# Store and load order on SyncE in the first stage of a fused Mamba and mixture-of-experts layer

## What is computed

```python
xn = _layernorm(x, axis=-1)
proj = jnp.einsum('bld,ed->ble', hidden_states, in_proj_w)
x, gate = jnp.split(proj, 2, axis=-1)
...                                   # causal convolution of x over 4 taps
xc = jax.nn.silu(xc + conv_b[None, :, None])
ssm = jnp.einsum('bld,ed->ble', xt, x_proj_w)
ts, Bm, Cm = jnp.split(ssm, [DT_RANK, DT_RANK + D_STATE], axis=-1)
...
y = y * jax.nn.silu(gate)             # after the scan
# router
logits = x @ gate_w.T
scores = jax.nn.softmax(logits, axis=-1)
topk_w, topk_i = jax.lax.top_k(scores, K)
...                                   # slot lists: which tokens each expert takes
```

## Time and profile before

| | |
|---|---|
| median of 3 runs | 1425.2 us (1420.97 to 1434.94) |
| profiled execution | 1420.89 us, its span 1418.7 us |
| mean granted PE clock | 0.971 |
| PE busy | 1317.4 us, 93% |
| DVE busy | 1083.4 us, 76% |
| ACT busy | 895.9 us, 63% |
| POOL busy | 880.8 us, 62% |
| DMA | 304.87 MB, mean 215 GB/s |

### The profile page before, as it was taken

The page is one execution under the profiler, slowest core; times in us unless marked ns, Lnnn a source line. Parts: engine busy times, 40 slices in busy tenths (PEclk is TensorE's granted clock), DMA queues, the critical chain, the costliest instruction groups (busy, mean ns, idle before and its releaser), DMA issues.

```text
span 1418.7 us, 53995 instructions
## 1 busy us (share of the span) xinstructions
PE 1317.4 (93%) x21895; PEld 813.1 (57%) x21895; DVE 1083.4 (76%) x1259; ACT 895.9 (63%) x1912; POOL 880.8 (62%) x523
## 2 busy tenths in 40 slices
PE   5898988769999999999999999999999869999998
PEld 3666656535555545555455555455554558787876
DVE  4688798749999979999789899889999255545554
ACT  3746554467878878887787878677786133333333
POOL 2444355269898978989789898888989130303030
PEclk9999999869999999999899999999999989999999
DMA  7152527558999999999889999989898732313130
GB/s 282 64 211 78 197 79 274 179 160 264 307 258 297 274 287 273 275 301 267 270 258 278 293 263 304 274 265 294 262 300 244 267 131 68 111 54 124 42 136 30
DMA packets 129681, 304.87 MB, mean 215 GB/s; under 512 B 18448, under 2 KB 20240, under 8 KB 127824
## 3 DMA queue, kind: packets, MB, share of 16 engines
q1 hardware_dynamic: 121984, 285.13, 61.5%
q0 software_dynamic: 7632, 18.91, 6.6%
HBM read 213.65 MB, written 56.77 MB: 191 GB/s over the span
## 4 chain that ended last, share of the span: by engine, by line
PE 40%; issue 19%; POOL 15%; DMA 2%; DVE 1%; ACT 1%; POOLq 1%; SPq 0%; DVEq 0%; ACTq 0%
PE p_dBx L1324 9%; PE p_dBx L1257 8%; POOL h_times_C L880 7%; POOL C_bcast L880 5%; PE p_y L1273 3%; PE p_y L1335 3%; PE p_g L1335 3%; PE p_u L1335 3%; PE p_g L1243 3%; PE p_dt L1335 2%; PE p_u L1226 2%; PE p_g L1226 2%; POOL moe L860 2%; DMA w_down_pair<-in_sw_down 1%; PE p_dt L1206 1%
## 5 line engine op out<-in xcount | busy, mean ns | idle before, releaser
L945 DVE TENSOR_TENSOR_SCAN state<-dA,state_carry,p_dBx 128x512 f32<-128x512 f32 x512 | 626.5, 1266 | 78.3 <-PE p_dBx L1257 69.3
L1091 ACT ACTIVATE dA<-dt_blocks,A_par 128x512 f32<-128x512 f32 x512 | 338.7, 709 | 39.3 <-DMA dt_blocks<-step_rows 39.2
L880 POOL TENSOR_TENSOR h_times_C<-state,C_bcast 128x1024 f32<-128x1024 f32 x128 | 305.2, 2385 | 70.8 <-DVE state L945 68.9
L880 POOL TENSOR_TENSOR C_bcast<-state,C_bcast 128x1024 f32<-128x1024 f32 x128 | 319.6, 2780 | 22.4 <-DVE state L945 17.5
L1257 PEld LDWEIGHTS p_dBx<-B_diagonals,step_rows 64*32 64x32 f32 x16384 | 232.4, 106 | 162.8 <-issue 162.7
L1257 PE MATMUL p_dBx<-B_diagonals,step_rows 64*32 64x128 f32 x16384 | 303.6, 276 | 10.3 <-issue 9.5
L254 POOL TENSOR_TENSOR w_in_parts_lo<-C_bcast,w_in_parts_hi 128x512 fp32r<-128x512 f32 x64 | 88.9, 1391 | 142.0 <-ACT w_in_parts_hi L447 141.7
L1324 PE MATMUL p_dBx<-x_parts,shared_w_parts 128*128 128x512 f32 (+1 forms) x576 | 139.7, 404 | 17.3 <-DVE shared_w_parts L974 12.1
L895 POOL TENSOR_TENSOR step_rows<-step_rows 128x512 f32<-128x512 f32 x16 | 20.6, 1319 | 202.2 <-DMA step_rows<-moe 202.2
L1324 PEld LDWEIGHTS p_dBx<-x_parts,shared_w_parts 128*128 128x128 f32 (+1 forms) x576 | 105.2, 184 | 51.8 <-issue 20.5
L326 DVE SCALAR_TENSOR_TENSOR conv_out<-conv_in,conv_w,conv_out 128x512 f32<-128x512 f32 x96 | 91.1, 958 | 9.4 <-ACT conv_out L461 7.1
(11 more groups left out here) (172 smaller groups left out, 2035.4 us busy)
## 6 DMA issues: line engine op xcount, KB each, us to landing
w_gate_pair<-in_w_gate SPq DMA_DIRECT2D x32, 1408.0 KB
w_up_pair<-in_w_up SPq DMA_DIRECT2D x32, 1408.0 KB, 8.1
w_down_pair<-in_w_down SPq DMA_DIRECT2D x66, 512.0 KB
dt_blocks<-step_rows SPq DMA_DIRECT2D x512, 64.0 KB
w_down_pair<-in_w_down SPq DMA_DIRECT2D x33, 384.0 KB
g_d<-y_gated SPq DMA_DIRECT2D x33, 256.0 KB, 4.3
sz_d<-silu_gate SPq DMA_DIRECT2D x32, 256.0 KB, 2.0
xt_d<-conv_out SPq DMA_DIRECT2D x4, 2048.0 KB, 7.3
```

Source lines behind the costliest of these rows:

```text
L880: pool.tensor_tensor(hc[m][:, b, :, :], hb[:, q, :, :], Cb[:, NM * cp + GS * m:NM * cp + GS * m + GS, :], ALU.mult).then_inc(s_hc, 1)
L945: ins = dve.tensor_tensor_scan(hb[:, g % NBUF, s, :], dA[:, g % NBUF, s, :], pB[:, g % 2, :].rearrange("p (t s) -> p s t", s=GS)[:, s, :], ...
L1091: ins = act.activation(dA[:, q, s, :], dtr[:, u, b, :], ACT.Exp, scale=A[:, bass.ds(d, 1), GS * g + s:GS * g + s + 1].rearrange("p a b -> ...
```

## The change

Only the order of SyncE's instructions in stage 1 changes. In each chunk, the stores of gate tiles 0 and 1 are issued ahead of the wait for the scores, and those of tiles 2 and 3 behind the `xn_d` store. In the last chunk the gate weights' load follows the stores of tiles 2 and 3, where it stood ahead of the stores of tiles 0 to 3; the 16 transfers of C are issued four at a time behind the stores of gate tiles 4, 5, 6 and 7, where all 16 stood ahead of them; and the up weights' load is issued behind all of these, directly ahead of the wait for the last chunk's `xt_d` store, where it stood behind the store of gate tile 3.

```diff
             for c in range(NCH):
                 sp.wait_ge(s_xnT, c + 1)
                 sp.dma_start(io["xnT_d"][c], xnT[:, :, :]).then_inc(s_xTs, 16)
+                store_gates(c, range(2))
                 sp.wait_ge(s_sc, c + 1)
                 sp.dma_start(xn_v[c], xs[:, :, :]).then_inc(s_xns, 16)
+                store_gates(c, range(2, ND // 2))
                 if c == NCH - 1:
                     tile_in.load_gate(sp, 0)
-                store_gates(c, range(ND // 2))
+                for d in range(ND // 2, ND):
+                    store_gates(c, range(d, d + 1))
+                    if c == NCH - 1:
+                        sp.wait_ge(s_wlo, 2 * ND * c + X_TURN)
+                        for a in range(2 * (d - ND // 2), 2 * (d - ND // 2) + 2):
+                            keep["load_C"](sp, 0, a)
                 if c == NCH - 1:
                     sp.wait_ge(s_val, NCH)
                     tile_in.load_up(sp, 0)
-                    sp.wait_ge(s_wlo, 2 * ND * c + X_TURN)
-                    for a in range(ND):
-                        keep["load_C"](sp, 0, a)
-                store_gates(c, range(ND // 2, ND))
                 sp.wait_ge(s_xt, ND * c + ND)
```

## The result

The change makes the kernel slower by 0.3%: the median is 1429.54 us (1423.86 to 1433.88, 20 runs) against 1423.24 us (1417.73 to 1435.8, 20 runs) for the kernel before. The ratio, 1.0032 with a 95% interval of 1.0016 to 1.0048, is that of the means (1429.28 and 1424.66); the medians lie 6.3 us apart. The profiled execution has a span of 1425.1 us (before 1418.7) and took 1427.25 us.

A forecast was written before the change was run, and what follows sets the result against it. VectorE was taken to set stage 1's chunks and the last `xt_d` store its end: +2.4 - 3.9 + 4.1, less up to 0.5, put the barrier +2.4 us later. On the median that gave 1427.6, stated as 1427.5; range 1416 to 1434.

The forecast's parts named there:

- DVE, not PE, sets the chunk's length: Stage 1: DVE runs nearly without a gap, so PE's gain is worth only what DVE can use.
- Part 1, the wait for the root: Chunks 2 and 3: DVE's wait for the reciprocal root falls to 1.14 us, by 1.65 and 1.62; together -3.3 us.
- Part 1, four meetings instead of two: Chunks 1 to 3, conv 2 to 4: two more GpSimd subtractions delay DVE, 2 x 0.9 = +1.8 us, to +2.1.
- Part 1 as a sum: Chunks 1 to 3, early gate stores: +1.9, +0.25 and +0.3 us, together +2.4; ends -3.3 and +3.0.
- a stop of 3 us or more before the transposes: Sign to see in the profile after: PE without a stall at n = 9 but with this stop.
- Part 2, the last chunk: ACT's 8.19 us and DVE's wait for the ranks go: -3.9 us at the `xt_d` store; ends -1.2 and -5.3.
- Part 3, the load in front of the store: Last chunk: up weights' load ahead of the last `xt_d` store, +4.1 us on its landing; ends 0 and +8.1.
- C's transfers and the gate weights' load cost nothing: Last chunk, SyncE's queue: C transfers between stores and the load behind gate stores 2 and 3 add nothing on the path.
- A: Rival: DVE's meetings with POOL stay two per chunk; -3.6 us, 1421.6; chance 0.22.
- B: Rival: meetings stay two per chunk and the up weights' load is hidden; -7.7 us, 1417.5; chance 0.06.
- C: Rival: SyncE's issues become the last chunk's chain, +2 to +4 us more, together about +6, 1431; chance 0.16.
- D: Rival: ACT's wait is for something other than the gate store; only +4.1 us remains, 1429.3; chance 0.04.

The follow-up runs named there:

- runs 5 and 6: Kernel before and changed kernel, GpSimd's subtractions in chunks 1 to 3 replaced by zero fills: 171.1 and 165.3 us from first exponent-sum to last; no ratio.
- Run 7: Changed kernel plus 36 identity transposes on PE ahead of the transposes of each chunk after the first: ratio 1.003 to the kernel before.
- run 12: The kernel before, unchanged, profiled once more: 191.6 us from first exponent-sum to last, then 48.8 to the barrier; timed once, no ratio.
- run 3: Changed kernel with the up weights' load moved directly behind the gate weights' load: ratio 0.999 to the kernel before, barrier at 285.75 us.
- run 11: Kernel before with only the last chunk's gate stores 0 and 1 early and gate weights' load behind tiles 2 and 3: ratio 0.9973.
- run 10: Same kernel as run 4, timed again: ratio 0.9988 to the kernel before (0.9971 to 1.0005), barrier at 283.63 us.
- run 4: Changed kernel with the old order in chunks 1 to 3 and the up weights' load behind the gate weights' load: ratio 0.9972 to the kernel before.

## Why the prediction was right, and where its terms were off

The forecast was 1427.5 us, 2.3 above the median known then, and the barrier 2.4 us later. The measured shift is +0.32%, 4.6 us, 2.3 to 6.8 by its interval: slower by less than 1% and in the range, but twice the forecast, and the forecast is at the very end of the interval. In the profile the barrier moved 7.3 us, three times the 2.4 of the sum. In this pair of profiles all three terms were off in the same direction (by 2.5, 1.3 and 0.8 us), so nothing cancelled; the range of 18 us, wider than all of this, is what held. The sign and the mechanism were right. Step by step:

- **DVE, not PE, sets the chunk's length, and PE's gain is worth only what DVE can use.** Right. ScalarE's waits are gone and chunks 1 to 3 are longer.
- **Part 1, the wait for the root, -3.3.** Right: 1.12 us in chunks 2 and 3, where 1.14 was forecast, and unchanged in chunk 1.
- **Part 1, four meetings instead of two, +5.7 before that gain.** Right: conv 2 to 4 went to 10.58, 10.59 and 10.59 us from 8.74, 8.73 and 8.73, +1.85 each. That the delays come from GpSimd's reading instructions is supported by runs 5 and 6, which took them all away. An overlap isn't a delay of VectorE by itself, though: in the first chunk of the old order a third subtraction began at 57.45, just behind conv's last instruction (57.4). It took 1.81 us itself, instead of 1.28, and that conv instruction stayed at 0.75.
- **Part 1 as a sum, +2.4, measured +4.9 in the profile.** The missing 2.5 us is a term that the sum lacked. I had listed "a stop of 3 us or more before the transposes" among the signs to see, and put no price on it. Its price is the chain clock, transposes, `x_lo`, conv 7: in chunk 2, conv 7 +4.23 less the 3.4 that the ranks gave back, 0.8 us. Run 7 cut the chain and got 1.15, 0.83 and 0.79 us back by the end of conv 7, 2.8 in all. Of the 4.9, then, 2.8 is this chain, 1.6 is what the sum priced at 2.4 (run 7 against before, to the end of conv 7), and 0.5 came behind the third conv 7 and isn't explained. The stop and the level behind it stood already in the old rows, after the gate tile's stall, where the granted clock was 0.62 from 116.6 to 121.1 us; I should have asked of the new stop what I had seen of the old one.
- **Part 2, the last chunk, -3.9.** Right in sign, -2.6 by the first profile: from the last exponent-sum to the issue of `xt_d` it is 35.50 us, before 38.12. The ranks' wait is gone and conv 6 lost its meeting (2.31 instead of 3.22), as forecast. But the comparisons rose to 4.29 from 2.93 and conv 2 to 3.89 from 3.23, the latter not in my count; nor is it the change's, for conv 2 took 3.88 in run 12 too. Against run 12, 40.36 us to the issue of `xt_d`, the term is -4.9. The six runs at 43.7 to 44.1 from the last exponent-sum to the barrier put it at 2.5 to 5.1 against the two profiles of before. The forecast lies within.
- **Part 3, the load in front of the store, +4.1.** Right in mechanism, +4.9 in the landing. From run 3 to the change the barrier moved 5.0 us for this one move. That the store "has no slack", from a lead of 0.3 us over VectorE, decided it. The 0.2 to 0.5 that I took off for the last small store didn't come: SyncE still waited 0.5 us for it.
- **"C's transfers and the gate weights' load cost nothing."** Right for C's (run 11).
- **The rivals.** A (two meetings still) is out by conv's 10.59, B (load hidden) by the landing. C, SyncE as the chain, is out, though not by much: the `xt_d` store was issued 0.19 us behind the end of silu of tile 7 (276.62 + 0.63, 277.44), and 0.03 before, and SyncE had only just finished its load at 277.39. So the load's issue cost some 0.15 us there, not the 2 to 4 of C. D is out by the waits.

Conv 7's longest instruction, its first, began at 142.6 beside the subtraction that ran from 142.31 to 147.10 and took 5.09 us, where 0.75 is its own length: it was held to the end of the other. That is the stronger reading of the Trainium skill's rule of the shared ports (SBUF — State Buffer, Two separate sides), and the trace agrees with it here. The source view of conv's instructions in the change (ns, least, middle, most):

```profile
L329 DVE SCALAR_TENSOR_TENSOR conv_out<-conv_in,conv_w,conv_out x3: 1646/1655/5093, 142.6 to 149.4; 128x512 f32<-128x512 f32 x3
```

## What to carry to other kernels

A wait that is removed lets everything behind it run earlier, and the question is what it will run beside: here four GpSimd subtractions and one long one came to lie beside VectorE's busiest stretch, and removing 9.8 us of stall in three chunks (3.38, 3.19, 3.18) made them 4.9 us longer in the profile. Count the pairs of GpSimd and VectorE instructions that overlap before and after, and for each which began first, and follow every new stop of PE to the clock behind it and to who gets its result late. And on a queue that ends a stage, put nothing big in front of the store that is waited for; the edit without that, and in the last chunk alone (run 11, four lines), is faster than the kernel before by 0.1 to 0.5%, and so than the changed one.

## What the runs showed that I had not expected

- The same stall of PE is followed by another clock from chunk to chunk and from execution to execution. Behind stops of 2.9 us in the first chunk and 2.7 in the second of the kernel before, the next tile took 2.85 us (53.68 to 56.53) at a granted clock of 1.00, and 4.44 at 0.62; in run 10 it was the other way round. This is worth 1.4 us of a chunk where the root hangs on it (run 10, chunk 1).
- So a single profile places a stage's end within some 2 to 3 us only, which is as much as most terms of my sum: run 10's first three chunks were 2.7 us longer than run 4's, and run 12's last chunk 2.3 us longer than the first profile's.
- GpSimd's reads cost VectorE far more in this stage than the change does: with fills in chunks 1 to 3 the old order took 1401.2 us (run 5, timed once), where the kernel before has a median of 1422.3 on the same chip. As a fill is also the shorter instruction, this is a bound for what moving the low parts elsewhere could bring, not a measure of it.
